# A twelve-layer decoder on one core: the selected-experts layer rewritten, projections of one attention layer re-timed, maxima negated in the reduce

## The reference, cut to what matters

```
x1, x2 = x @ sw1.T + sb1, x @ sw2.T + sb2
shared = layernorm(silu(x1) * x2) * g + b, then @ sw3.T + sb3     # all 2048 tokens
xm     = x[index_b, index_t]                                      # 256 picked tokens
s, e   = sigmoid(xm @ sg.T + sgb), sigmoid(xm @ eg.T + egb)       # 1 and 8 scores
top1   = argmax(e + exp_bias);  w = softmax([s, e[top1]])
z      = layernorm(silu(xm @ ew1[n] + eb1[n]) * (xm @ ew2[n] + eb2[n])) * g2 + b2    # n of 8 experts, 64 wide
out    = shared;  out[index] = w0 * shared[index] + w1 * (z[top1] @ ew3[top1] + eb3[top1])
```

## Time and profile before

| | |
|---|---|
| time, median of 3 runs | 2374.45 us (2373.88 to 2378.79) |
| the profiled execution | 2378.78 us |
| its span, from the first to the last instruction | 2377.0 us |
| mean granted TensorE clock | 0.89 |
| PE, PEld, DVE, ACT, POOL busy | 84%, 50%, 61%, 47%, 27% of the span |
| layer 3, 722.5 to 931.0 | 208.5 us |
| layer 6, 1092.3 to 1445.4 | 353.1 us |
| layer 8, 1524.4 to 1642.6 | 118.2 us |
| layer 9, 1642.6 to 2032.3 | 389.7 us |

### The profile page before, as it was taken

One profiled execution on the slowest core, in us unless ns is written; L12 is line 12 of the kernel. 1 busy time (PEld: TensorE's weight loads), 2 busy tenths in 40 slices (PEclk: granted clock), 3 DMA queues, 4 the chain that ended last, 5 costly groups with the idle time before them and its releaser, 6 DMA issues. The chain is left out here.

```text
span 2377.0 us, 37476 instructions
## 1 busy us (share of the span) xinstructions
PE 2000.3 (84%) x12495; PEld 1195.5 (50%) x12495; DVE 1440.6 (61%) x3369; ACT 1108.8 (47%) x2808; POOL 647.4 (27%) x907
## 2 busy tenths in 40 slices
PE   6679999879995887666999996656899999599997
PEld 3434544434442554544666664435566666244444
DVE  6468899444433554684777765562666665477762
ACT  4325555534431665333555553220566666167762
POOL 7434342100003432101111105301434432333312
PEclk9769999889995888887999998865999999689996
DMA  1133321386642330001000001101000000434321
GB/s 34 30 95 70 76 51 42 74 189 144 143 99 69 80 77 19 23 0 37 1 2 1 2 2 31 33 1 42 1 2 2 1 2 1 105 77 86 76 48 26
DMA packets 126321, 112.29 MB, mean 47 GB/s; under 512 B 61193, under 2 KB 98996, under 8 KB 123828
## 3 DMA queue, kind: packets, MB, share of 16 engines
q1 hardware_dynamic: 92852, 108.84, 19.8%
q10 hardware_dynamic: 33280, 1.05, 0.7%
HBM read 93.67 MB, written 15.20 MB: 46 GB/s over the span
## 5 line engine op out<-in xcount | busy, mean ns | idle before, releaser
L957 DVE TENSOR_REDUCE L_xattn_mx<-L_xattn_psS 128x1 f32<-128x512 f32 x512 | 326.2, 683 | 116.1 <-PE L_xattn_psS L1082 112.1
L1192 ACT ACTIVATE L_xattn_PT<-L_xattn_psT 128x512 f32<-128x512 f32 x512 | 283.2, 600 | 95.1 <-PE L_xattn_psT L1094 89.5
L603 ACT ACTIVATE L_attn_pr<-L_attn_psS,L_attn_negm 128x256 f32<-128x256 f32 (+1 forms) x512 | 222.0, 446 | 103.1 <-DVE L_attn_negm L403 68.0
L1082 PE MATMUL L_xattn_psS<-L_xattn_KR,L_xattn_QR 72*128 72x512 bf16 x512 | 212.8, 421 | 43.2 <-DVE L_xattn_mx L957 21.1
L401 DVE TENSOR_REDUCE L_attn_mx<-L_attn_psS 128x2 f32<-128x512 f32 x256 | 164.9, 686 | 114.3 <-PE L_attn_psS L512 114.2
L1094 PE MATMUL L_xattn_psT<-L_xattn_QR,L_xattn_KR 75*128 75x256 bf16 x1024 | 198.3, 279 | 3.8 <-ACT L_xattn_PT L1192 1.6
L1108 PE MATMUL L_xattn_psO<-L_xattn_PT,L_xattn_V 128*32 128x256 f32 x2048 | 193.1, 400 | 3.2 <-ACT L_xattn_PT L1192 1.1
L2068 DVE TENSOR_TENSOR L_ffn_act<-L_ffn_act,L_ffn_cwb 128x512 f32<-128x512 f32 x128 | 86.7, 690 | 129.9 <-ACT L_ffn_act L2198 106.0
L512 PE MATMUL L_attn_psS<-L_attn_qk 64*128 64x256 f32 x1024 | 146.6, 404 | 11.6 <-ACT L_attn_pr L603 11.6
L2133 PE MATMUL L_ffn_psU<-L_ffn_hT,L_ffn_wup 128*128 128x512 f32 x256 | 133.3, 612 | 13.6 <-ACT L_ffn_act L2198 13.6
L2198 ACT ACTIVATE L_ffn_act<-L_ffn_psU 128x512 f32<-128x512 f32 (+1 forms) x132 | 78.5, 597 | 135.7 <-PE L_ffn_psU L2133 131.8
(11 more groups left out here) (553 smaller groups left out, 3952.1 us busy)
## 6 DMA issues: line engine op xcount, KB each, us to landing
L_ffn_cwb<-L_ffn_weights_by_expert SPq DMA_DIRECT2D x64, 512.0 KB, 7.8
L_xattn_KR<-L_xattn_k_parts SPq DMA_DIRECT2D x96, 192.0 KB
L_xattn_QR<-L_xattn_q_parts SPq DMA_DIRECT2D x32, 288.0 KB
L_xattn_k_parts<-L_xattn_ks SPq DMA_DIRECT2D x48, 128.0 KB, 2.4
L_xattn_ctxT<-in_ctx SPq DMA_DIRECT2D x24, 192.0 KB, 2.4
L_attn_QR<-L_attn_q_parts SPq DMA_DIRECT2D x16, 288.0 KB
L_attn_KR<-L_attn_k_parts SPq DMA_DIRECT2D x48, 96.0 KB
L_xattn_q_parts<-L_xattn_qs SPq DMA_DIRECT2D x48, 64.0 KB, 2.1
```

What stands on the lines that cost most here:

```text
L603: ins = nc.scalar.activation(pr[n % 3][:, r, t, 0:width], psS[(2 * n + r) % 3][:, t, 0:width], ACT.Exp, bias=negm[:, n % 4, t, r:r + 1], s ...
L957: nc.vector.reduce_max(mx[:, b % 2, u, hd:hd + 1], psS[n % 2][:], AX.X).then_inc(s_used, 1)
L1082: ins = nc.tensor.matmul(psS[n % 2][:, i * keys:(i + 1) * keys], QR[b % NB][0:PAIR, hd, t * P:(t + 1) * P], KR[b % NB][0:PAIR, hd, :], sta ...
L1192: nc.scalar.activation(PT[n % NPT][:, 2 * u:2 * u + 2], psT[i % NPS][:], ACT.Exp).then_inc(exp_ready, 1)
```

## The change

Layer 8 is written anew. Weights are packed on the host, SP issues ten loads on six semaphores, the index loads first. Norms are made in groups of four tiles; ACT writes h and the normalised shared tiles. Project adds its bias by a matmul of one row. The one-hot choice is turned, spread by PE over 128 partitions and multiplied into the picked tokens (`mask_inputs`), so the hidden sums of all experts add up in one bank, 128 wide a tile. The same is done behind the norm (`mask_hidden`), and gain and shift are applied after the turn. The weights come from tanh instead of sigmoid and exp. The number of picks of a token comes from comparing the indices on DVE (`same`, `rdup`), and the kept share rides as column 129 of the scatter. The orders of PE, DVE and ACT interleave shared and expert work.

In layer 3 T of batches 2 and 3, Q, K, V, A and O and the staging of batches 1 to 3 move; in layers 1, 3 and 10 the split parts have two buffers and their semaphores go by the parity of the batch (`LAST` of layer 1 is two steps less, both empty).

In layers 6 and 9 the reduce writes the negated maximum, with a count for each of the two heads; the scale moves into wq (layer 6, by ACT after the loads) or into the query half of the rotary tables (layer 9), which are twice as long and not broadcast.

```diff
-                    nc.vector.tensor_tensor(dst[:], bank[:], tab[:, None, :].to_broadcast((P, 2, S)), ALU.mult).then_inc(free, 1)
+                    nc.vector.tensor_tensor(dst[:], bank[:], tab[:], ALU.mult).then_inc(free, 1)
...
-                    link.mark(nc.vector.reduce_max(mx[:, n % 4, :, r], psS[g % 3][:], AX.X))
-                link.wait()
-                nc.vector.tensor_scalar(negm[:, n % 4], mx[:, n % 4], -SCALE, None, ALU.mult).then_inc(negm_ready, 1)
+                    nc.vector.tensor_reduce(negm[:, n % 4, :, r], psS[g % 3][:], AX.X, ALU.max, negate=True).then_inc(negm_ready, 1)
...
+            if causal:
+                pe.wait_ge(wq_scaled, 1)
...
-                pe.wait_ge(negm_ready, n + 1)
                 for r in range(2):
+                    pe.wait_ge(negm_ready, 2 * n + r + 1)
...
+                nc.scalar.mul(wq[:], wq[:], SCALE).then_inc(wq_scaled, 1)
...
-                act.wait_ge(negm_ready, n + 1)
                 for r in range(2):
+                    act.wait_ge(negm_ready, 2 * n + r + 1)
...
-    LEAD, PREP, STAGE, EARLY, DVE_SPLITS = (HH + 6, 38, 7, 3, 2) if from_ctx else (HH + 10, 52, 9, 6, 3)
+    LEAD, PREP, STAGE, EARLY, DVE_SPLITS = (HH + 6, 38, 7, 3, 2) if from_ctx else (HH + 10, 52, 9, 4, 3)
     LATE_V = H + 7
-    APART, BACK = (4, 6) if from_ctx else (7, 8)
+    APART, BACK = (4, 6) if from_ctx else (9, 9)
     DEPTH = 60.0
-    FIRST, LAST = -LEAD, NH + (16 if head_major else 10)
+    FIRST, LAST = -LEAD, NH + (16 if head_major else BACK + 2)
     NO = 2 if head_major else 1
...
-        for i, kind in ((0, "K"), (2, "T"), (3, "Q")) if from_ctx else ((0, "T"), (2, "Q"), (4, "K")):
+        for i, kind in ((0, "K"), (2, "T"), (3, "Q")) if from_ctx else ((0, "T"), (4, "Q"), (6, "K")):
             jobs[at + i * (b > 0)].append((kind, b, 0))
-        jobs[max(H * b - LATE_V, FIRST) if from_ctx else at + 6 * (b > 0)].append(("V", b, 0))
+        jobs[max(H * b - LATE_V, FIRST) if from_ctx else at + 8 * (b > 0)].append(("V", b, 0))
...
-        qs, ks = sb("qs", [P, PARTS, S], BF16), sb("ks", [P, PARTS, keys], BF16)
+        qs, ks = ([sb(f"{n}{i}", [P, PARTS, w], BF16) for i in range(2)] for n, w in (("qs", S), ("ks", keys)))
...
-            wait(eng, q_staged, 16 * PARTS * b)
-            split(eng, link, qf, qs, q_split)
+            wait(eng, q_staged[b % 2], 16 * PARTS * (b // 2))
+            split(eng, link, qf, qs[b % 2], q_split)
...
-                    wait(act, staged, 16 * PARTS * b)
+                    wait(act, staged, 16 * PARTS * (b // 2))
...
-            for dst, src in loads:
-                sp.dma_start(dst, src).then_inc(loaded, 16)
+            for dst, src, done in ((idx_row[:].rearrange("p a m -> p (a m)"), wide("idx_row", 2 * M), idx_loaded),
+                                   (idx_col[:].rearrange("p a t -> p (a t)"), d[f"{pre}_idx_col"], idx_loaded),
+                                   (wx[:], d[f"{pre}_wx"], w_loaded), (sb12[:], rows(d[f"{pre}_sb12"]), w_loaded),
+                                   (gates[:], wide("gates", NEG + E), gates_loaded),
+                                   (ew12[:], d[f"{pre}_ew12"], e_loaded), (e8[:], d[f"{pre}_e8"], e_loaded),
+                                   (w3[:], d[f"{pre}_w3"], w3_loaded), (gb[:], d[f"{pre}_gb"], w3_loaded),
+                                   (ew3[:], d[f"{pre}_ew3"].rearrange("e f d -> (e f) d").rearrange("(n p) d -> p n d", p=P), e3_loaded)):
+                sp.dma_start(dst, src).then_inc(done, 16)
 
...
+            def root(mom, eps, r, nmr, c, n):
+                link(nc.gpsimd.tensor_scalar(eps[:, c], mom[:, c, 1], LN_EPS, None, ALU.add))
+                link(nc.gpsimd.tensor_tensor(r[:, c], eps[:, c], m.half[:, 0:n], ALU.pow))
+                link(nc.gpsimd.tensor_tensor(nmr[:, c], mom[:, c, 0], r[:, c], ALU.mult))
+                return nc.gpsimd.tensor_scalar(nmr[:, c], nmr[:, c], -1.0, None, ALU.mult)
...
+            def shared(b):
                 dve.wait_ge(silu_ready, b + 1)
                 i = slice(TB * b, TB * (b + 1))
-                link.mark(nc.vector.tensor_tensor(u[:, i], u[:, i], x12[:, i, F:], ALU.mult))
+                nc.vector.tensor_tensor(u[:, i], u[:, i], psX[b % 2][:, 0:TB * 2 * F].rearrange("p (t k f) -> p t k f", t=TB, k=2)[:, :, 1], ALU.mult).then_inc(u_ready, 1)
+                dve.wait_ge(u_ready, b + 1)
+                for j in batch(b):
+                    link.mark(nc.vector.bn_stats(ust[:, j], u[:, j]))
+                link.wait()
+                for j in batch(b):
+                    nc.vector.bn_aggr(umom[:, j], ust[:, j]).then_inc(u_moments, 1)
...
+            def mask_inputs(k):
+                dve.wait_ge(mask_ready, k + 1)
+                nc.vector.tensor_tensor(xm[:, 2 * k:2 * k + 2], psE[k % 2][:].rearrange("p (e m) -> p e m", e=2),
+                                        xpT[:, None, :].to_broadcast((P, 2, M)), ALU.mult).then_inc(xm_ready, 1)
...
+            moments(0)
+            moments(1)
...
+            picks(0)
+            moments(2)
+            picks(1)
+            moments(3)
+            picks(2)
+            picks(3)
...
-            link(nc.vector.tensor_tensor(E1, E1, we.mean[:, :, None].to_broadcast(shape), ALU.subtract))
...
-            nc.vector.tensor_tensor(E1, E1, fl(oh[:])[:, :, None].to_broadcast(shape), ALU.mult).then_inc(ez_ready, 1)
...
+            for k in range(E // 2):
+                mask_inputs(k)
+            shared(1)
...
+                    nc.vector.tensor_scalar(ez[:, t, k], eu[:, t], emom[:, t, 0:1], er[:, t:t + 1], ALU.subtract, ALU.mult).then_inc(ez_ready, 1)
+            shared(3)
+            for k in range(2):
+                mask_hidden(k)
+            shared(4)
...
+                link(nc.vector.tensor_scalar(keep[:, i], part[:, :, D], 1.0, None, ALU.add))
+                dve.wait_ge(so_ready, b + 1)
+                for t in range(TB):
+                    j = TB * b + t
+                    nc.vector.scalar_tensor_tensor(tmp[:, t], so[:, j], keep[:, j:j + 1], part[:, t, 0:D], ALU.mult, ALU.add).then_inc(tmp_ready, 1)
+                dve.wait_ge(tmp_ready, TB * (b + 1))
+                nc.vector.tensor_tensor(m.x[:, b], m.x[:, b], tmp[:], ALU.add).then_inc(x_done, 1)
...
+                    nc.tensor.matmul(at, ones[:], sb12[:], start=True, stop=False)
+                    ins = nc.tensor.matmul(at, hT[:, i], wx[:, 0:2 * F], start=False, stop=True)
...
+            def spread_masks(k):
+                wait(pe, xm_ready, k - 1)
+                for j in range(2):
+                    e = 2 * k + j
+                    ins = nc.tensor.matmul(psE[k % 2][:, j * M:(j + 1) * M], m.identb[0:E, e:e + 1].to_broadcast((E, P)), ohTb[:], start=True, stop=True)
+                ins.then_inc(mask_ready, 1)
...
+                        ins = nc.tensor.matmul((psC if t == 0 else psG)[:, 0:2 * F], xm[:, e, t * P:(t + 1) * P], ew12[:, e], start=False, stop=(e == E - 1))
...
+                        ins = nc.tensor.matmul(psE[b % 2][:, i % TB * (D + 1):(i % TB + 1) * (D + 1)], spread[:, t, i * P:(i + 1) * P], picked[:, t], start=(t == 0), stop=(t == MT - 1))
...
+            for b in range(B):
+                turn(b)
+                gather(b)
+                if b == 4:
+                    project(0)
+                if b == 6:
+                    project(1)
...
-                    ins = nc.tensor.matmul(psG[:, 2 * i:2 * (i + 1)], spread[:, t, i * P:(i + 1) * P], picked_out[:, t, D:], start=(t == 0), stop=(t == MT - 1))
...
+            spread_masks(0)
+            spread_masks(1)
+            hidden(0)
+            spread_masks(2)
+            hidden(1)
+            spread_masks(3)
+            hidden(2)
+            hidden(3)
+            project(3)
+            pair_masks(0)
+            pair_masks(1)
+            project(4)
...
+            turn_shared(0)
+            turn_shared(1)
+            project(5)
+            shared_out(0)
...
+            shared_out(1)
+            project(6)
+            turn_shared(2)
+            project(7)
+            turn_shared(3)
+            shared_out(2)
+            shared_out(3)
+            scatter(0)
+            turn_shared(4)
+            scatter(1)
+            shared_out(4)
+            turn_shared(5)
...
+            nc.scalar.activation(warm[:], m.half[:, 0:1], ACT.Silu)
...
+            nc.scalar.activation(sc[:], gl[:], ACT.Tanh, scale=0.5).then_inc(tanh_ready, 1)
+            silu(1)
...
+            nc.scalar.activation(dif[:], dif[:], ACT.Tanh, scale=0.5).then_inc(wt_ready, 1)
```

511 lines of the change are left out of this document (300 added, 211 removed).

## The result

Four interleaved runs of each kernel gave 2376.62 us before (2373.88 to 2383.59) and 2321.24 us after (2315.46 to 2327.52): a ratio of 0.9765, 95% interval 0.9736 to 0.9794, that is 56 us saved, 49 to 63. The forecast was 2310.5, 64 saved; it was 10.7 us too low. The profiled execution took 2315.46 us around a span of 2313.7.

What follows compares the result with a forecast made beforehand. Layers run serially: 6 and 9 matmul-bound, 8 a row of mutually waiting stages, 3 held by issue order. Terms -48 - 18 + 0.5 + 1.5 = -64 from 2378.78 gave 2314.8, less 4.3: 2310.5 us; 8-in-10 range 2291 to 2332.

Steps and rivals of the forecast that it cites:

- so I add 3.5 for the low level: Layer 8: 3.5 us added to the 66.5 us sum because PE stays sparse in B and C.
- the term of 4.8: Layer 8, part A: first four gather batches run at the low clock level, adding 4.8 us.
- 8.5 at step 0: Layer 3: batch 1 begins near 760.5 instead of 767.25 and PE's 2.3 us wait goes, saving 8.5 us.
- Now M is ahead of Q, so its rows leave about 5 us sooner, and the ACT wait goes: Layer 3 after step 0: max rows no longer follow POOL's work on Q; seven batches at 2.7 us are 19.
- the term of 9.5: Layer 3 after step 0: half of the 19 us taken, as early batches still share SP's queue.
- rival 1: Layer 3's staging stays the bound, rows queue behind more issues; layer 3 gives 2 us: 2326 us, chance 0.15.
- the 1.0 I took: Layer 9: 1.0 us gained at the ramp from waiting for each half separately.
- Both signs that I had named for being wrong: Wrong if TensorE's clock in layer 8 stays near 0.6, or if SP's queue sets layer 3.
- (2): Layer 8 stays at the low clock level in A and D: 14 to 16 us more, 2325 us, chance 0.15.
- (3): Layer 8: tanh between silus costs four table loads of 1.28 us, about 4 on the chain: 2315 us, chance 0.10.
- (4): Both better bounds are met, 60 us for layer 8 and 27 saved in layer 3: 2292 us, chance 0.03.
- (5): Layers 6 and 9: half-wise waits break PE's stream and its clock falls: 2380 us and up, chance 0.02.

Runs made afterwards that it cites:

- with fillers: Changed kernel plus 8 groups of six unread bf16 matmuls ahead of PE's waits in layer 8: 2310.43 us, ratio 0.9723; layer 8 63.8 us.
- layer3_order_only: Kernel before with only layer 3's new order of steps, without second buffers for the split parts: 2364.31 us, ratio 0.9943.

## Why the prediction was right, and where it was off

**Layer 8: -48 forecast, -44 measured.** The parts of my sum against the rows of after:

| part | forecast | after | with fillers |
|---|---|---|---|
| A, to the last gather | 22.8 | 19.3 | 19.8 |
| B, to the first silu of the hidden sums | 9.7 | 13.7 | 9.9 |
| C, to the end of the chosen output | 13 | 16.6 | 12.4 |
| D, the rest | 21 | 24.5 | 21.6 |
| low level besides | 3.5 | in the parts | |
| sum | 70 | 74.1 | 63.7 |

B, C and D come out within 0.6 us of the forecast once fillers stand in PE's queue, and the terms were priced at durations of the high level. B and C then run at 1.00; D still has 8 us at 0.60 in it, so its agreement is in part luck. The step that was mis-sized is "so I add 3.5 for the low level". It measured 10.9 us (13.7 + 16.6 + 24.5 against 9.9 + 12.4 + 21.6). In B it also turned the order of the engines round: I put the hidden matmuls under DVE's masks, and four masks of 0.69 us with their hops are 3.2 us; at the low level a pair of experts takes PE 2.3 us (1.22 and 1.06 for its two halves), and with its masks it comes every 2.5, so DVE and ACT waited for PE. A was shorter mainly because only the first gather (1.91 us) and two turns, not the first four batches, ran at the low level: the term of 4.8 measured 1.4. So the sum of 70 came within 4 us of 74 because A was 3.5 too long and the low level 7.4 too short. The loads: their wait of 12.88 us went, as forecast. DVE had the indices 17.1 us into the layer before, 8.8 with ten loads and the indices last, 3.4 with the indices first. SP's issues of the 27 loads took 14.8 us, those of the ten 4.4. So, as far as this run can tell, 8.3 us of the 13.7 came from the number of loads and 5.4 from their place, and the place costs the layer 4.1.

**Layer 3: -18 forecast, -10.5 here, -13.0 by the means.** The first half stands: 8.5 at step 0 forecast, 9.6 measured, batch 1 at 37.5 us instead of 38. (The two terms named for it, 6.75 and 2.3, make 9.05 and not 8.5. And the 2.3 were put down to the second buffer of the parts, while the kernel without it, layer3_order_only, has its first exponential at 41.6 us, as the others.) The second failed, at the step "Now M is ahead of Q, so its rows leave about 5 us sooner, and the ACT wait goes": the term of 9.5 measured 3.2. M ahead of Q only moves the turn of the maxima. From ACT's negation to the first issue of the rows an undisturbed set takes 2.6 to 2.7 us. Five of the sixteen took 5.8 to 7.2 before, and four take 6.2 to 7.7 after, since the rows still cannot leave before SP has spread the next batch (rival 1's mechanism). And when they do leave at once, they land in the middle of that spread and the single buffer is not free in time, which neither my case nor a rival had. Two buffers gave 7.4 us in the old order and 6.7 in the new one, by the means.

**Layers 6 and 9: +0.5 and +1.5 forecast, +0.2 and -2.5 measured.** The longer tables are there: PE's first matmul starts 15.6 us into layer 9 instead of 14.5, 1.1 later (forecast 1.2); over all executions the means are 15.6 and 14.8. The table load is there too, but it costs nothing, since it lies in ACT's idle time ahead of the first exponential:

```profile
1603.49 1.28 ACT L605 ACT_TABLE_LOAD   x1
...
1615.24 0.47 ACT L605 ACTIVATE L_attn_pr<-L_attn_psS,L_attn_negm 128x256 f32<-128x256 f32 x1 [10.46 <-DVE L_attn_negm L401]
```

The kernel with the new layer 8 alone, which has the load and not the other edits, took 389.2 us there: 0.5 under before's 389.7. The ramp gave more than the 1.0 I took: the first exponential is 31.4 us in against 30.9, but the fifth is 34.5 against 35.4 and the last 375.8 against 378.1. Some of it is won at the ramp, then, as the waits by halves would have it, and some later, which no run here explains.

**Layers 1 and 10, and the median.** Zero, as far as it can be seen (layer 10 varies by 8 us over the fourteen executions). My start was the span of the profiled execution, and in the profiled one of after layers 0 and 10 were 2.4 and 2.1 us shorter without any edit that acts on them: by spans the change is 63.3 us, by the timed ratio 56. The means of the layers sum to 43.6 + 13.0 + 2.5 - 0.2 = 58.9. Of the 10.7 us by which the forecast was too low, 2.2 are the start: the median of before came out at 2376.62 instead of 2374.45.

**How much of it was luck.** Against 58.9 the forecast of 64 is 5 us off, but its terms are off by more and in both directions: layer 8 by 4.4 and layer 3 by 5.0 too much, layers 6 and 9 by 4.3 too little. Both signs that I had named for being wrong came in part: the clock in layer 8 is 0.72 over the whole layer (0.61 before) but 0.69 behind the last gather, and SP's queue does hold layer 3's rows back.

**The rivals.** (1) is half true: its mechanism works, but the layer gave 13 us instead of its 2. (2), the low level in A and D, came in B, C and the first half of D, for 10 us instead of 14 to 16. (3) falls: tanh between silus cost no load. (In the kernel before, silu, sigmoid and exp cost a load of 1.28 us each in layer 8, at 1560.23, 1570.87 and 1604.06, and sigmoid and silu one each way in layer 2, at 459.03 and 462.10; the earlier trace rows shows only the first of these.) The Trainium skill, "ScalarE: Activation LUTs", "Table sets: the hidden batching unit", lists tanh with exp and with sigmoid and asks to batch calls by set. Its list has no silu; if silu's set had no tanh, this order would have paid four switches. The trace shows one load of 1.28 us in the whole layer: here silu and tanh ran from the same loaded table. (4) and (5) did not come; layers 6 and 9 kept their clocks of 0.98 and 0.96.

## What to carry to other kernels

A term made of durations at the high clock level holds only where PE is granted it. Price a sparse stretch at both levels; where PE is in front of the other engines, a few matmuls with no reader may pay for themselves. When a wait for a buffer ends on a DMA, add up the whole way round (write, issue, landing) and compare it with the time between two uses. Take the landing from where the other transfers run, not from a quiet stretch. If the way is longer, an earlier issue or another queue moves the wait, and a second buffer removes it. A DMA issued from a busy engine's queue is not paid for in busy time but in what stands behind it.

## What the runs showed of the hardware that was not expected

PE was granted 0.50 for 18 us while it was busy 17.45 of them. With 48 small matmuls ahead of its waits it was granted 1.00 for 24 us where it had been 0.66 and 0.68, and only 8 us at 0.60 were left of the low stretch. The rows of 8 heads, three DMAs of one partition each, landed 1.1 us after their last issue where the DMA engines were 5% busy, and up to 5.6 us after it where they were 62% busy with the spread of the next batch. Issuing three of them took SP 1.96 to 2.05 us, GpSimd 1.65 and ACT 1.95. Silu and tanh ran from one loaded table. An unchanged layer at the start of the program took 96.5 to 97 us at a granted clock of 0.96, about 99.4 at 0.91, or 102.4 to 103.1 at 0.88 to 0.90 from one execution to the next, which is more than several of the edits here are worth.
